# A rebuilt head for a three-stage attention and expert kernel: load order, one table set for the roots, and the first batch ahead of most queries

## The reference

```python
x = x + xattn(ctx, ctx, layernorm(x), Wv, Wk, Wq, Wo, bo)     # 16 heads of 8, 257 keys per batch
x = x + attn(layernorm(x), ...)                               # 8 heads, latent keys, rotary parts with
                                                              #   angles that need sigmoid(raw_delta)
x = x + moe(layernorm(x), w_router, w_gate, w_up, w_down)     # 8 experts, top 2
# xattn: k = keys @ Wk.T, v = values @ Wv.T, q = query @ Wq.T, per head softmax(q k / sqrt(8)) v, then @ Wo.T + bo
```

## Time and profile before

| | |
|---|---|
| time, median of 3 runs | 480.22 us (479.7 to 482.32) |
| the profiled execution's own time | 479.78 us |
| its span, first to last instruction | 477.9 us |
| busy share of the span | PE 88%, PEld 71%, DVE 67%, ACT 62%, POOL 43% |
| mean granted TensorE clock | 0.964 |

### The profile page before, as it was taken

The page is one execution under the profiler, slowest core; times in us unless marked ns, Lnnn a source line. Parts: engine busy times, 40 slices in busy tenths (PEclk is TensorE's granted clock), DMA queues, the critical chain, the costliest instruction groups (busy, mean ns, idle before and its releaser), DMA issues. The chain is left out here.

```text
span 477.9 us, 13886 instructions
## 1 busy us (share of the span) xinstructions
PE 419.8 (88%) x4037; PEld 338.5 (71%) x4037; DVE 321.6 (67%) x954; ACT 296.4 (62%) x875; POOL 206.0 (43%) x482
## 2 busy tenths in 40 slices
PE   0889999999999999999988799988977999999950
PEld 0567677777767777777756687887876888888850
DVE  5368888888888888888875678888471333333325
ACT  3588888888888888888875878742122232232234
POOL 0545555545555454555531100000005777777740
PEclk9999999999999999999999999999579999999995
DMA  5345111111111111111000000001007766766626
GB/s 159 78 152 202 37 42 33 44 33 38 39 33 44 33 38 38 33 43 33 11 2 1 0 2 1 1 1 67 23 7 245 216 201 212 217 189 216 185 63 240
DMA packets 31999, 38.86 MB, mean 81 GB/s; under 512 B 5952, under 2 KB 29184, under 8 KB 31712
## 3 DMA queue, kind: packets, MB, share of 16 engines
q1 hardware_dynamic: 29472, 33.35, 22.8%
q0 software_dynamic: 2496, 5.12, 3.6%
HBM read 33.80 MB, written 4.65 MB: 80 GB/s over the span
## 5 line engine op out<-in xcount | busy, mean ns | idle before, releaser
L398 ACT ACTIVATE PR<-PS,nmax 128x257 f32<-128x257 f32 x256 | 117.9, 474 | 30.5 <-DVE nmax L586 30.5
L586 DVE TENSOR_REDUCE nmax<-PS 128x1 f32<-128x257 f32 x256 | 90.5, 416 | 20.0 <-PE PS L861 19.9
L868 PE MATMUL PS<-I,PR 128*128 128x128 f32 x512 | 67.3, 275 | 0.0
L348 POOL DMA_INDIRECT XG<-x_table,IDX x39 | 37.8, 970 | 58.1 <-DVE IDX L789 46.5
L868 PEld LDWEIGHTS PS<-I,PR 128*128 128x128 f32 x512 | 58.7, 143 | 0.3 <-issue 0.3
L302 POOL TENSOR_TENSOR O<-OM 128x64 f32<-128x64 f32 x64 | 20.4, 319 | 84.1 <-DVE OM L609 84.1
L795 DVE TENSOR_TENSOR H<-PS,SG 128x384 f32<-128x384 f32 x39 | 21.7, 558 | 49.9 <-PE PS L1081 48.8
L398 ACT ACTIVATION_READ_ACCUMULATOR PR<-PS,nmax 128x1 f32 x256 | 51.9, 203 | 0.0
L529 ACT ACTIVATE SG<-PS 128x384 f32<-128x384 f32 x39 | 19.1, 490 | 49.5 <-PE PS L1081 49.5
L883 PE MATMUL PS<-PT,KV 128*32 128x128 f32 x1024 | 41.6, 280 | 6.2 <-DVE PT L591 5.8
L861 PE MATMUL PS<-KV,QM 32*128 32x257 f32 x512 | 45.8, 427 | 1.3 <-ACT PR L398 0.7
(11 more groups left out here) (194 smaller groups left out, 837.7 us busy)
## 6 DMA issues: line engine op xcount, KB each, us to landing
CR<-ctxT SPq DMA_DIRECT2D x64, 128.0 KB, 2.1
GC<-w_gate SPq DMA_DIRECT2D x39, 192.0 KB
UC<-w_up SPq DMA_DIRECT2D x39, 192.0 KB, 3.4
Y<-y_table SPq DMA_DIRECT2D x4, 512.0 KB, 5.2
DW<-w_down SPq DMA_DIRECT2D x1, 1536.0 KB, 6.1
NAMES<-lanes SPq DMA_DIRECT2D x1, 1344.0 KB, 8.3
X<-x SPq DMA_DIRECT2D x4, 256.0 KB, 3.5
x_table<-xe SPq DMA_DIRECT2D x4, 256.0 KB, 2.4
```

The costliest lines, as they stand in the source:

```text
L348: g.indirect_dma_start(XG[:, s % XRING, :], None, x_table[:, :], bass.IndirectOffsetOnAxis(IDX[:, s:s + 1], 0)).then_inc(gathered[s % XRIN ...
L398: a.activation(PR[:, j % 2, gr, 0:S], src, ACT.Exp, bias=bias, accum_out=rsum[:, j % 2, gr:gr + 1]).then_inc(exped, 1)
L586: v.tensor_reduce(nmax[:, gr:gr + 1], bank[gr][:, 0:S], AX.X, ALU.max, negate=True).then_inc(max_ready, 1)
L868: ins = t.transpose(bank[4 + ch][:, 128 * gr:128 * gr + 128], PR[:, j % 2, gr, KC * ch:KC * ch + KC], I128[:, :])
```

## The change

- SyncE loads `X` first. The four rotary constants are issued by ScalarE, on its own queue.
- The one semaphore for six weights becomes three: `in_wkv` (`WkS`, `WvS`), `in_wq` (`WqS`, `HM`), `in_wo` (`boB`, `WoS`).
- The square root and VectorE's reciprocal become a logarithm and an exponential on ScalarE with set 6 (`root_inverse`), which the other norms use already. Set 6 is loaded right after the sines.
- The second half of the rotary constants (nine small VectorE operations) moves behind `maxima(0)`.
- TensorE begins with `keep_busy(12)`, projects batch 0's keys ahead of the queries, adds `keep_busy(4)`, and scores batch 0 after two quarters of queries. Quarters 2 and 3 follow `score(0)`, and `absorb()` stays behind all four. The queries use banks 4, 5 and 7 in turn.
- GpSimd adds the bias a quarter at a time, each after one of `step(0)` to `step(3)`; VectorE waits for `x_biased` ahead of the loop and no longer ahead of `step(0)`.
- Contexts 8 to 11 are issued ahead of `DW`, 12 to 15 behind it.

```diff
@@ SyncE
-            sp.dma_start(small[:, 0, :], bc(raw_delta.unsqueeze(0), [128, 16])).then_inc(in_rot, 16)
-            for dst, src in ((cpos, cos_pos), (spos, sin_pos), (BM, own_sequence)):
-                sp.dma_start(dst[:, :], src).then_inc(in_rot, 16)
             for n in range(4):
                 sp.dma_start(X[:, 4 * n:4 * n + 4, :], x[512 * n:512 * n + 512, :].rearrange("(t p) d -> p t d", p=128)).then_inc(in_x[n], 16)
             sp.dma_start(I128[:, :], ident).then_inc(in_ident, 16)
             sp.dma_start(CL[:, :], ctx_last).then_inc(in_last, 16)
-            for dst, src in ((WqS, wq), (WkS, wk), (WvS, wv), (WoS, wo), (HM, head_mask)):
-                sp.dma_start(dst[:, :], src).then_inc(in_wqk, 16)
-            sp.dma_start(boB[:, :], bc(bo.unsqueeze(0), [128, D])).then_inc(in_wqk, 16)
+            for dst, src in ((WkS, wk), (WvS, wv)):
+                sp.dma_start(dst[:, :], src).then_inc(in_wkv, 16)
...
+            load_ctx(0, 0)
+            for dst, src in ((WqS, wq), (HM, head_mask)):
+                sp.dma_start(dst[:, :], src).then_inc(in_wq, 16)
@@ GpSimd
-            for n in range(4):
-                s = slice(4 * n, 4 * n + 4)
+            for k in range(4):
+                step(k, k, 0)
+                s = slice(4 * k, 4 * k + 4)
                 g.tensor_tensor(X[:, s, :], X[:, s, :], bc(boB[:, :].unsqueeze(1), [128, 4, D]), ALU.add).then_inc(x_biased, 1)
             g.wait_ge(q_scaled, 4)
-            for k in range(4):
-                step(k, k, 0)
@@ ScalarE
+            a.dma_start(small[:, 0, :], bc(raw_delta.unsqueeze(0), [128, 16])).then_inc(in_rot, 16)
+            for dst, src in ((cpos, cos_pos), (spos, sin_pos), (BM, own_sequence)):
+                a.dma_start(dst[:, :], src).then_inc(in_rot, 16)
...
-            a.wait_ge(in_wqk, 96)
-            a.wait_ge(ln_step, AT_1 + 7)
-            a.activation(std[:, :], var[:, :], ACT.Sqrt).then_inc(std_ready, 1)
+            a.add_instruction(mybir.InstLoadActFuncSet(name=nc.get_next_instruction_name(), act_func_set_id=6, ins=[], outs=[]))
+            root_inverse(a, AT_1, 0)
...
-            for k in range(2):
-                keys_and_values(k, k)
-            a.add_instruction(mybir.InstLoadActFuncSet(name=nc.get_next_instruction_name(), act_func_set_id=6, ins=[], outs=[]))
+            keys_and_values(0, 0)
+            normed_out(0)
+            scale_queries(0)
+            keys_and_values(1, 1)
+            normed_out(1)
+            scale_queries(1)
             exps(0, 0)
+            normed_out(2)
             keys_and_values(2, 2)
+            scale_queries(2)
+            normed_out(3)
+            scale_queries(3)
@@ VectorE
-            v.wait_ge(x_biased, 4)
             for k in range(4):
                 step(k, k, 0)
+            v.wait_ge(x_biased, 4)
@@ TensorE
+            keep_busy(12, 0)
             t.wait_ge(in_last, 16)
-            t.wait_ge(in_wqk, 96)
+            t.wait_ge(in_wkv, 32)
...
-            for k in range(2):
-                project(k, k, 0)
+            project(0, 0, 0)
+            keep_busy(4, 0)
+            turn_x(0)
+            t.wait_ge(in_wq, 32)
+            project_queries(0)
+            project(1, 1, 0)
+            turn_x(1)
+            project_queries(1)
+            score(0, 0)
+            turn_x(2)
+            project(2, 2, 0)
+            project_queries(2)
+            turn_x(3)
+            project_queries(3)
             t.wait_ge(q_scaled, 4)
-            score(0, 0)
-            project(2, 2, 0)
             absorb()
```

More of the change, by code:

```diff
@@ L240, in load_ctx @@
                 sp.dma_start(CR[:, j, :], ctxT[:, bass.ds(k * S, 2 * KC)]).then_inc(in_ctx[j], 16)
-            for j in range(4):
+            load_ctx(0, 0)
+            for dst, src in ((WqS, wq), (HM, head_mask)):
+                sp.dma_start(dst[:, :], src).then_inc(in_wq, 16)
+            for j in range(1, 4):
                 load_ctx(j, j)
+            sp.dma_start(boB[:, :], bc(bo.unsqueeze(0), [128, D])).then_inc(in_wo, 16)
+            sp.dma_start(WoS[:, :], wo).then_inc(in_wo, 16)
             for dst, src in ((uqT[:, :, :], w_uqT), (ukT[:, :, :], w_ukT), (uvT[:, :, :], w_uvT), (woutS, w_out)):
@@ L249, in _ @@
                 load_ctx(4 + j, j)
+            for j in range(4):
+                load_ctx(8 + j, j)
             sp.dma_start(DW[:, :], w_down).then_inc(in_moe, 16)
+            for j in range(4):
+                load_ctx(12 + j, j)
             sp.dma_start(wrT[:, :], w_router).then_inc(in_moe, 16)
@@ L254, in _ @@
             sp.dma_start(NAMES[:, :], bc(lanes.unsqueeze(0), [128, lanes.shape[0]])).then_inc(in_names, 16)
-            with sp.Fori(2, T) as i:
+            with sp.Fori(4, T) as i:
                 for j in range(4):
@@ L379, in _ @@
             a.activation(LP[:, :, :].rearrange("p c b -> p (c b)"), bank[6][:, 0:2 * B], ACT.Copy).then_inc(last_copied, 1)
[L380 to L384, removed]
             def keys_and_values(k, j):
@@ L575, in _ @@
             norm_sums(v, AT_1)
-            v.wait_ge(std_ready, 1)
-            v.reciprocal(rstd[:, :], std[:, :]).then_inc(ln_step, 1)
-            v.wait_ge(ln_step, AT_1 + 8)
+            v.wait_ge(rstd_ready, 1)
             for t in range(T):
@@ L626, in _ @@
             maxima(0)
+            v.wait_ge(rot_act, 3)
+            v.scalar_tensor_tensor(out=sm(1), in0=sm(3), scalar=-2.0, in1=sm(5), op0=ALU.mult, op1=ALU.mult).then_inc(rot_step, 1)
+            v.scalar_tensor_tensor(out=sm(2), in0=sm(3), scalar=2.0, in1=sm(3), op0=ALU.mult, op1=ALU.mult).then_inc(rot_step, 1)
+            v.wait_ge(rot_step, 7)
+            v.tensor_scalar(sm(2), sm(2), 1.0, None, ALU.subtract).then_inc(rot_step, 1)
+            v.wait_ge(rot_step, 8)
+            v.tensor_tensor(cosT[:, :], cpos[:, :], sm(2), ALU.mult).then_inc(rot_step, 1)
+            v.tensor_tensor(sm(0), spos[:, :], sm(1), ALU.mult).then_inc(rot_step, 1)
+            v.tensor_tensor(sinT[:, :], spos[:, :], sm(2), ALU.mult).then_inc(rot_step, 1)
+            v.tensor_tensor(sm(3), cpos[:, :], sm(1), ALU.mult).then_inc(rot_step, 1)
+            v.wait_ge(rot_step, 12)
+            v.tensor_tensor(cosT[:, :], cosT[:, :], sm(0), ALU.subtract).then_inc(rot_step, 1)
+            v.tensor_tensor(sinT[:, :], sinT[:, :], sm(3), ALU.add).then_inc(rot_step, 1)
             v.wait_ge(absorbed, 1)
@@ L818, in _, with keep_busy @@
             t.wait_ge(in_ident, 16)
+            def keep_busy(n, bk):
+                for m in range(n):
+                    t.matmul(bank[bk][:, 0:128], I128[:, :], I128[:, :], start=True, stop=True)
             def turn_x(n):
+                if n >= 2:
+                    t.wait_ge(ln_copied, n - 1)
                 for m in range(4):
                     t.wait_ge(ln_out, 4 * n + m + 1)
-                    ins = t.transpose(bank[n][:, 128 * m:128 * m + 128], XL[:, 4 * n + m, :], I128[:, :])
+                    ins = t.transpose(bank[(4, 7)[n % 2]][:, 128 * m:128 * m + 128], XL[:, 4 * n + m, :], I128[:, :])
                 ins.then_inc(ln_turned, 1)
@@ L825, in project_queries @@
                 t.wait_ge(ln_copied, n + 1)
-                t.matmul(bank[n][:, :], WqS[:, :], XLT[:, 512 * n:512 * n + 512], start=True, stop=True).then_inc(q_ready, 1)
+                if n >= 1:
+                    t.wait_ge(q_scaled, n)
+                t.matmul(bank[5][:, :], WqS[:, :], XLT[:, 512 * n:512 * n + 512], start=True, stop=True).then_inc(q_ready, 1)
+            keep_busy(12, 0)
             t.wait_ge(in_last, 16)
-            t.wait_ge(in_wqk, 96)
+            t.wait_ge(in_wkv, 32)
             t.matmul(bank[6][:, 0:B], WkS[:, :], CL[:, :], start=True, stop=True)
             t.matmul(bank[6][:, B:2 * B], WvS[:, :], CL[:, :], start=True, stop=True).then_inc(last_proj, 1)
[L831 to L835, removed]
             def absorb():
@@ L923, in _ @@
             t.wait_ge(absorbed_out, 3)
-            def keep_busy(n, bk):
-                for m in range(n):
-                    t.matmul(bank[bk][:, 0:128], I128[:, :], I128[:, :], start=True, stop=True)
             def turn_normed(n):
```

32 lines of the change are left out of this document (10 added, 22 removed).

## The result

The changed kernel takes 486.99 us (median of 6 runs, 485.11 to 489.01) against 480.61 us (6 runs, 479.7 to 482.87). The ratio on record is 1.0111, 95% interval 1.0082 to 1.014 (the two medians alone give 1.013): slower, by 5.3 us. On the 480.22 us that the forecast started from this makes 485.6 us, inside the range of 481.2 to 486.6; the median itself lies 0.4 us above that range. The profiled execution took 488.42 us with a span of 486.6 us, 8.7 us more than the span before. The two traces thus lie some 3 us further apart than the runs as a whole.

What follows compares the result with a forecast made beforehand. The loop has no engine with room to catch up, so the head counts by when the pipeline starts. Profiled 479.78 + 2.6 (later `score(1)`) + 1.3 (bias) = 483.7, median 0.44 above: 484.1 us, range 481.2 to 486.6.

Steps and rivals of the forecast that it cites:

- Quarters 2 and 3 behind `exps(0)`: Head: their copies follow `exps(0)` on ScalarE and `absorb()` follows both, putting `score(1)` at 30.1 instead of 27.52, 2.6 us later.
- The bias: Loop: VectorE waits 1.5 us for GpSimd's fourth addition, behind `sum_heads(2)`; 1.3 us stay. Rival that it is hidden: chance 0.14.
- The norm earlier by 2.5 us: Head: with `X` loaded first, normalised tiles start at 10.5 us instead of 13.01.
- I take 0.3, since they are small and issued in the same microsecond: Loads: delay of the constants from travelling beside `X`, taken as 0.3 us, bounds 0 and about 2.5.
- behind all of `X`: Loads: upper bound for the constants, landing after the whole of `X`, about 2.5 us later.
- all it issues next comes 1.87 us sooner: SyncE: `X` is issued from 0.75 instead of 2.62, so everything after it also comes 1.87 us sooner.
- The third part: Norm: from the variance's end to the first tile takes 0.6 us instead of 1.92.
- TensorE is late to the first quarter: Head: fillers, last keys and `project(0)` put its copy at 14.9, a wait of 2.7 us. Rival, not late: 0.13.
- T0: TensorE: end of the first twelve fillers, put at 11.3 us (11.0 to 12.1).
- I take 3.5 us: TensorE: time from the first matmul to the clock's rise without gaps, bounds 3 and 5.5; fillers then take 4.5 us.
- The clock falls in the new gaps: Rival, TensorE in the head: thin work between quarters lowers the clock, +2 us, 486.1 us in all; chance 0.15.
- At nothing: Parts put at no cost: small operations behind `maxima(0)`, one table load less, later contexts, the head's weights.

Runs made afterwards that it cites:

- e4: Changed kernel with the four rotary constants issued by SyncE ahead of `X` again; ratio 1.015 to the kernel before.
- e5: Changed kernel with 12 more filler matmuls in three TensorE gaps behind the first scores; ratio 1.014 to the kernel before.
- e11: e2 plus one small VectorE operation ahead of the loop; 486.82 us, ratio 1.014 to the kernel before.
- e3: Changed kernel with all four query quarters ahead of batch 0's projection and scores again, no second fillers, old banks; ratio 1.000 to the kernel before.
- e7: e6 with the four rotary constants issued by SyncE ahead of `X`; ratio 0.997 to the kernel before.
- e1: Changed kernel without the two runs of filler matmuls in the head; ratio 1.016 to the kernel before.
- e6: Changed kernel's loads and roots, with query order and bias of before and no fillers; ratio 1.007 to the kernel before.
- e9: e7 with 4 filler matmuls between the last keys and the first turns; ratio 0.998 to the kernel before.
- e10: e9 plus one small VectorE operation ahead of the loop; 478.07 us, ratio 0.9955 to the kernel before.
- e2: Changed kernel with GpSimd's bias additions and VectorE's wait back where they stood before; 487.0 us, ratio 1.014 to the kernel before.
- e12: Kernel before, with the last small VectorE operation of the rotary constants moved from the head behind the loop; ratio 1.003 to the kernel before.

## Why the prediction was right, and where not

- **Direction and reason held.** It was slower because the head ended later, and the loop kept the delay. The forecast had 3.9 us; the timed runs show 5.3, the two traces 8.7. That the forecast came so near the runs is in part luck: in the traces it missed 2.6 us at the first copy and 1.8 us of a slow clock. (Its chances for slower and same add up to 0.72 and 0.20, not 0.71 and 0.21.)
- **Quarters 2 and 3 behind `exps(0)`, 2.4 us of the forecast's 2.6:** right. First copy to `score(1)` took 15.30 us against a forecast of 15.2, before 12.83 (15.0 in e4, e5 and e11, where `absorb()` was not slow). e3 undoes it.
- **The bias, 1.3 us:** right, 1.68 us of idle time and 1.58 us at the end (8.71 less 7.13, of which 1.41 at batch 6). e3 keeps it, e11 is without it.
- **The norm earlier by 2.5 us: wrong.** Tiles came at 13.50, 0.5 later than before. The step that failed is "I take 0.3, since they are small and issued in the same microsecond": the first exponential started at 7.46, 3.6 us later than before and beyond the bound of 2.5. The upper case, "behind all of `X`", is what happened. e4 and e7 give 2 to 2.7 us back for the constants' queue. Nor did "all it issues next comes 1.87 us sooner" hold for the landings: `X` took 5.2 us where it had taken 3.5. The third part held: from the variance's end to the first tile it took 0.53 us (12.97 to 13.50), forecast 0.6, before 1.92. The miss did no harm to the sum, as the forecast let the norm's gain end in a wait for TensorE; e4, with the norm early, shows that it does. The Trainium skill (DMA: Bandwidth & Descriptors, "Queues, rings and completion order") says that a semaphore's increment lands only after every earlier write of that DMA engine, across its queues; the 5.3 us of `BM`, against 1.7 when it went ahead of `X`, agree, though no run here tells this from a shared bandwidth.
- **TensorE is late to the first quarter:** right in kind, mis-sized. T0 was 13.66, forecast 11.3 with 12.1 as its top. The identity landed at 8.38, not 6.8 ("1.87 us sooner that is 6.8": it took 5.4 us where 3.9 were taken over), and the fillers took 5.28 us, at the top of their bounds, not 4.5 (the time up to the clock's rise, "I take 3.5 us", was a choice that no row showed). The first copy was at 17.53, forecast 14.9. And what I called the fillers' delay is only partly theirs: e1 shows that without them the copy of the last keys, queued behind the norm on ScalarE, holds the same place.
- **The clock falls in the new gaps, +2, chance 0.15:** it happened in this trace, and cost 1.81 us between `score(1)` and batch 2, 0.86 in e4 and e11, nothing in e1. The granted clock was 1.00 from 28.0 to 31.4 us with TensorE busy 2.26 of 3.40, and 0.50 behind. The Trainium skill (TensorE: Matmul & The Clock Gate, "A second HAM failure mode: psum-queue depth-cycling") has this as a danger of short, frequent idles. The stretch agrees in kind, with gaps of 0.7 to 1.5 us; e5, with the gaps filled, shows no fall, but neither does e1, so that the gaps are the cause is likely and not shown.
- **At nothing:** the roots from set 6, the split semaphores, the later constants and contexts cost nothing to be seen by batch 2; e3 has them all, and its batch 2 is within 0.07 us of the kernel before. A cost of the roots shows only with the early bias: without the reciprocal the loop's code starts one instruction sooner, and its rounds are longer (e6, e7, e9 against e10).

The sum by the marks: 2.84 (first copy) + 2.47 (order) + 1.81 (clock) + 1.58 (bias) = 8.7 us; the forecast had 0.2 + 2.4 + 0 + 1.3. By e3, the new order with its second fillers is the cause of 7.05 of them at batch 2, since it also brings the late copy and the gaps.

## What to carry to other kernels

To start one batch early is worth something only if what the pipeline starts on comes earlier; here the mark was batch 1's scores, and work that used to lie beside the first exponentials was put behind them. Read the program order of every engine at the seam: what stands behind the new early step, and which copy stands behind a wait that has become late. Small loads that other engines need first go ahead of a bulk load, not beside it (e7 against e6: 1.69 us at `score(1)`).

## What the runs showed of the hardware that I had not expected

- A loop's speed hung on how many VectorE instructions stand ahead of it. One VectorE operation more or less ahead of it decided a gap of 0.21 us a round, and with it whether a round took 14.00 us (196.07 over 14 rounds before) or 14.12 (197.73 in e12), 1.7 us in all (e2, e6, e7, e9, e12 with it; e10, e11 without). Why (the fetch of instructions is a guess) was not tried. Two kernels that differ ahead of a loop can so differ in it.
- Small loads on a second queue did not pass a bulk load on the first: 3.2 to 5.3 us to land instead of 1.7 to 2.1. The bulk load itself took 5.2 us instead of 3.5, but it was then also the first load of the program, and no run parts the two.
- The same 24 filler instructions took 4.2 to 5.3 us from run to run (4.23 in e4, 4.29 in e11, 5.28 in the changed kernel), as the high level was reached earlier or later (read from their lengths). In e10, four fillers and then the turns:

```profile
10.15 2.02 PE L827 MATMUL PS<-I 128*128 128x128 f32 x8
11.97 1.52 PE L831 MATMUL PS<-I,XL 128*128 128x128 f32 x8
...
25.32 0.72 PE L865 MATMUL PS<-KV,QM 32*128 32x257 f32 x8 [0.58 <-DVE Wvo L636]
```
